# A graph network on one core: the attention layer's last sum and layer norm, taken in seven steps inside the dense stage

## The reference, cut to what matters

```python
x = _layernorm(x + _L0_gnn_ref(x, ..., src, dst, edge_type_40))     # attention
x = _layernorm(x + _L1_gnn_ref(x, edge_index, W_l, W_r))             # mean of the neighbours
x = _layernorm(x + _L2_gnn_ref(x, edge_index, edge_weight, ...))     # three graph convolutions
x = _layernorm(x + _L3_gnn_ref(x, edge_index, edge_attr_64, ...))    # filtered messages
```

## Time and profile before

| | us |
|---|---|
| median of three runs | 9683.03 |
| the profiled execution's own time | 9686.6 |
| its span, from the first to the last instruction | 9685.1 |
| TensorE matmuls busy | 7655.3 (79%) |
| VectorE busy | 4238.9 (44%) |
| ScalarE busy | 3170.6 (33%) |
| GpSimd busy | 5527.7 (57%) |
| mean granted TensorE clock, as a share of full speed | 0.874 |

### The profile page before, as it was taken

The page is one execution under the profiler, slowest core; times in us unless marked ns, Lnnn a source line. Parts: engine busy times, 40 slices in busy tenths (PEclk is TensorE's granted clock), DMA queues, the critical chain, the costliest instruction groups (busy, mean ns, idle before and its releaser), DMA issues. The chain is left out here.

```text
span 9685.1 us, 154107 instructions
## 1 busy us (share of the span) xinstructions
PE 7655.3 (79%) x38400; PEld 4785.0 (49%) x38401; DVE 4238.9 (44%) x9974; ACT 3170.6 (33%) x5260; POOL 5527.7 (57%) x5296
## 2 busy tenths in 40 slices
PE   1598888888888576665655899999999888888786
PEld 0354444444444365555554444444444656656564
DVE  6887777774443366666666100000000323323223
ACT  0012234566555476655554000000000233233322
POOL 4788888877776000000000667777775477777775
PEclk6899999999999766666666999999999999999998
DMA  4223445566666443333222899999999322222222
GB/s 108 76 90 118 147 150 186 196 215 234 212 213 211 153 134 119 114 104 100 93 90 68 311 338 335 339 335 343 324 355 329 116 77 77 77 78 77 78 77 66
DMA packets 563179, 1661.59 MB, mean 172 GB/s; under 512 B 115313, under 2 KB 312029, under 8 KB 519494
## 3 DMA queue, kind: packets, MB, share of 16 engines
q1 hardware_dynamic: 324442, 1129.76, 33.5%
q0 software_dynamic: 206976, 473.99, 16.5%
q10 hardware_dynamic: 31536, 54.94, 1.6%
HBM read 1174.46 MB, written 483.82 MB: 171 GB/s over the span
## 5 line engine op out<-in xcount | busy, mean ns | idle before, releaser
L907 PE MATMUL wide<-ring 128*128 128x392 bf16 x14112 | 2498.4, 339 | 501.3 <-DVE ring L837 260.9
L527 POOL DMA_INDIRECT z_got<-z_table,z_idx x1568 | 2114.5, 1349 | 596.4 <-issue 430.9
L907 PEld LDWEIGHTS wide<-ring 128*128 128x128 bf16 x14112 | 1407.8, 100 | 1591.7 <-issue 822.8
L1589 POOL DMA_INDIRECT l_rows<-h_table,l_recs x1568 | 1558.9, 994 | 630.1 <-issue 477.5
L1498 POOL DMA_INDIRECT sorted_recs<-dn_rec_in,type_f x1568 | 1520.0, 969 | 654.0 <-issue 470.9
L1042 POOL DMA_DIRECT2D rows<-z_edges x196 | 103.5, 528 | 2049.3 <-PE wide L362 1838.3
L1401 PE MATMUL wide<-stream,X 128*128 128x512 f32 (+1 forms) x2548 | 1045.5, 570 | 63.0 <-DMA stream<-c_dense 58.8
L373 PE MATMUL wide<-rows,onehot 128*128 128x130 f32 x3904 | 869.7, 411 | 245.8 <-DVE A L390 245.8
L373 PEld LDWEIGHTS wide<-rows,onehot 128*128 128x128 f32 x3904 | 805.3, 314 | 304.3 <-DVE A L390 304.3
L373 PE MATMUL wide<-l_rows,l_onehot 128*128 128x128 f32 x3904 | 587.2, 313 | 357.2 <-DVE X L391 357.2
L1688 DVE TENSOR_TENSOR l_rows<-l_filters,l_rows 128x1024 f32<-128x1024 f32 x196 | 240.2, 1226 | 1330.7 <-DMA l_rows<-h_table,l_recs 1313.2
(11 more groups left out here) (252 smaller groups left out, 8327.1 us busy)
## 6 DMA issues: line engine op xcount, KB each, us to landing
stream<-w_dense SPq DMA_DIRECT2D x252, 1792.0 KB
stream<-c_dense SPq DMA_DIRECT2D x84, 1792.0 KB
z_edges<-z_got POOLq DMA_DIRECT2D x196, 528.0 KB
rows<-z_edges POOLq DMA_DIRECT2D x196, 528.0 KB, 3.8
dst_bc<-in_dst_row SPq DMA_DIRECT2D x196, 512.0 KB, 3.7
c_dense<-A SPq DMA_DIRECT2D x49, 1568.0 KB
w_dense<-A SPq DMA_DIRECT2D x49, 1568.0 KB
c_dense<-H SPq DMA_DIRECT2D x49, 1568.0 KB
```

The source lines that it names most:

```text
L527: e.indirect_dma_start(out=z_got[:, s, t, :], out_offset=None, in_=z_table, in_offset=bass.IndirectOffsetOnAxis(ap=z_idx[:, s, t:t + 1], a ...
L907: ins = e.matmul(banks[:, bass.ds(to[v], 1), int(m > 0), 0:WC].rearrange("p a x -> p (a x)"), lhsT=slots[:, k, m * P:(m + 1) * P], rhs=slo ...
L1589: e.indirect_dma_start(out=rows[:, k, t, :], out_offset=None, in_=h_table, in_offset=bass.IndirectOffsetOnAxis(ap=recs[:, k, t, R_DST:R_DS ...
```

## The change

The two blocks of point 3 are gone. Their work is done in the dense block, by VectorE ahead of its own loop over the chunks, in seven pieces of seven node blocks. A piece is split in two: `add_attention(s)` goes up to the variance and raises `s_spread`; ScalarE takes the square root of that piece's seven variances and raises `s_root`; `normalize_x(s)` waits for that, normalizes the seven blocks and raises `s_x0`. `add_attention(s)` stands before `normalize_x(s - 1)`. In chunk 0 alone TensorE waits for `s_x0` before each of its seven steps. The square roots stand on ScalarE behind the first four loads of records and before its first copy of transposes (L1443 of the kernel before). SP's list and GpSimd's are unchanged; both begin with the dense block, and so now before this work and not after it. `rden` moves to the memory of the dense stage.

```diff
-        rden = sb("rden", [P, NB], of=edges)
-        A0 = A_(SW_)
-        with nc.Block() as block:
-            @block.vector
-            def _(e):
-                e.tensor_scalar(rden[:, :], A0[:, :, F], TINY, None, ALU.max)
-                e.tensor_scalar(rdeg[:, :], A0[:, :, MW], 1.0, None, ALU.max)
-                e.drain()
-                e.reciprocal(rden[:, :], rden[:, :])
-                e.reciprocal(rdeg[:, :], rdeg[:, :])
-                e.drain()
-                for b in range(NB):
-                    e.scalar_tensor_tensor(out=Xv[:, b, :], in0=A0[:, b, 0:F], scalar=rden[:, b:b + 1],
-                                           in1=Xv[:, b, :], op0=ALU.mult, op1=ALU.add)
-                e.drain()
-                e.tensor_tensor(Xv, Xv, bias["L0_gnn_bias_w"][:, :].unsqueeze(1).to_broadcast([P, NB, F]), ALU.add)
-                e.drain()
-        layernorm("l0n", None)
         release_semaphores()
...
+        s_spread, s_root, s_x0 = sem("dn_spread"), sem("dn_root"), sem("dn_x0")
...
                         for k in range(KQ):
                             b = s * KQ + k
+                            if i == 0 and k == 0:
+                                e.wait_ge(s_x0, s + 1)
...
+                    if i == 0:
+                        for s in range(NS):
+                            e.wait_ge(s_spread, s + 1)
+                            e.activation(rstd[:, s * KQ:(s + 1) * KQ], rstd[:, s * KQ:(s + 1) * KQ], ACT.Sqrt
+                                         ).then_inc(s_root, 1)
...
+                def add_attention(s):
+                    bs = slice(s * KQ, (s + 1) * KQ)
+                    for b in range(s * KQ, (s + 1) * KQ):
+                        e.scalar_tensor_tensor(out=Xv[:, b, :], in0=A0[:, b, 0:F], scalar=rden[:, b:b + 1],
+                                               in1=Xv[:, b, :], op0=ALU.mult, op1=ALU.add)
+                    e.drain()
+                    e.tensor_tensor(Xv[:, bs, :], Xv[:, bs, :],
+                                    bias["L0_gnn_bias_w"][:, :].unsqueeze(1).to_broadcast([P, KQ, F]), ALU.add)
+                    e.drain()
+                    for b in range(s * KQ, (s + 1) * KQ):
+                        e.bn_stats(stats[:, b, :], Xv[:, b, :])
+                    e.drain()
+                    for b in range(s * KQ, (s + 1) * KQ):
+                        e.bn_aggr(mv[:, b, :], stats[:, b, :])
+                    e.drain()
+                    e.tensor_scalar(rstd[:, bs], mv[:, bs, 1], EPS, None, ALU.add).then_inc(s_spread, 1)
+
+                def normalize_x(s):
+                    bs = slice(s * KQ, (s + 1) * KQ)
+                    e.wait_ge(s_root, s + 1)
+                    e.reciprocal(rstd[:, bs], rstd[:, bs])
+                    e.drain()
+                    for b in range(s * KQ, (s + 1) * KQ):
+                        ins = e.tensor_scalar(Xv[:, b, :], Xv[:, b, :], mv[:, b, 0:1], rstd[:, b:b + 1],
+                                              ALU.subtract, ALU.mult)
+                    ins.then_inc(s_x0, 1)
+
...
+                add_attention(0)
+                for s in range(1, NS):
+                    add_attention(s)
+                    normalize_x(s - 1)
+                normalize_x(NS - 1)
+                e.drain()
                 for c in range(NCH):
```

More of the change, by code:

```diff
@@ L1299, in build_program @@
         dvar = sb("dvar", [P, 4], of=dense)
+        rden = sb("rden", [P, NB], of=dense)
+        A0 = A_(SW_)
         agg_bank, lin_bank, own_bank, turn_x, turn_r = (bank[0], bank[1]), bank[2], bank[3], bank[4], bank[5]
@@ L1467, in normalize @@
                     return ins
+                def add_attention(s):
[23 more added lines that the diff above has]
+                    ins.then_inc(s_x0, 1)
+                e.tensor_scalar(rden[:, :], A0[:, :, F], TINY, None, ALU.max)
+                e.tensor_scalar(rdeg[:, :], A0[:, :, MW], 1.0, None, ALU.max)
+                e.drain()
+                e.reciprocal(rden[:, :], rden[:, :])
+                e.reciprocal(rdeg[:, :], rdeg[:, :])
+                e.drain()
+                add_attention(0)
[3 more added lines that the diff above has]
+                normalize_x(NS - 1)
+                e.drain()
                 for c in range(NCH):
```

## The result

The changed kernel takes 9647.5 us (median of five runs, 9630.5 to 9656.54) against 9685.68 us of the kernel before in the same session (five runs). The ratio is 0.9961, with a 95% interval of 0.995 to 0.9972: 38.2 us or 0.4% faster.

The account below looks back on a forecast made before the run. TensorE was taken to bound the dense stage, idle while VectorE worked alone before it. Chunk 0 ending at 5368.0 instead of 5406.2 us gains 38.2, so 9683.0 - 38.2 = 9645 us, range 9638 to 9662.

Parts of the forecast that it names:

- The start of the dense block: After the attention layer's last add (L390): dense block and its loads start 1.12 us later, at 5304.3 us.
- One piece: VectorE's work on seven node blocks: 7.5 us, 5.4 for `add_attention` and 2.1 for `normalize_x`; seven pieces 52.5 us.
- When X comes free: `s_x0` first rises at 5318.5 us, then every 7.5 us to the sixth at 5356.0; the seventh at 5358.1.
- What TensorE makes of it: Chunk 0: steps of 6.0 us, the first 2.5 longer, four pauses of 0.5 to 1.5 us, end at 5368.0.
- What moves with it: Loads, records and scatter start 48.5 us earlier; nothing is late, though GpSimd pauses some 20 us.
- The price not shown: VectorE's pieces beside GpSimd's scatters and full DMAs: cost between nothing and 31 us, taken as nothing.
- The range: Total time from 9638 us, if VectorE set no pace, to 9662 us, covering one late fetch and parts of rivals.
- rival 4: Dense stage: loads cannot follow TensorE's earlier pace and the gain is given back; up to 9664 us, chance 0.03.
- Rival 1: Chunk 0: pauses keep TensorE at the low clock; gain only 3.5 us, 9680 us, chance 0.02.
- Rival 2: VectorE's pieces: GpSimd's scatters block VectorE for up to 31 us; gain 11.1 us, 9672 us, chance 0.03.
- Rival 3: VectorE's pieces stall on late instruction fetches: one 9659 us (chance 0.04), two 9674 (0.02), four 9703 (0.03).

Follow-up runs that it names:

- x4: Changed kernel, but VectorE's work left uncut in 49-block instructions inside the dense block, with TensorE waiting once for all of it: 9681.41 us, interval 93.6 us.
- x3: Changed kernel, but TensorE waits before its first matmul of chunk 0 until all seven pieces are done: 9682.17 us, interval 100.0 us.
- x6: Changed kernel, but each piece is normalized right behind its own add, not after the next one's: 9646.45 us, interval 63.9 us.
- x7: Changed kernel, but GpSimd begins its scatter only after the last piece is done: 9660.89 us in one run, interval 65.2 us.
- x5: Changed kernel, with the seven bn_stats of each piece done three times over to lengthen the pieces: 9669.63 us, interval 87.0 us.
- x8: Changed kernel, with the bias row added by GpSimd in the attention stage and the last normalize done by ScalarE: 9655.56 us, interval 55.5 us.
- x9: Changed kernel, with only the normalize moved to ScalarE, on a slower chip: 10993.1 us, ratio 0.998 to the kernel before, interval 72.6 us.
- x11: The kernel of x9 again, on a chip like the first: 9657.58 us, ratio 0.9958 to the kernel before, interval 56.1 us.
- x10: The changed kernel run again on the slower chip of x9: 10953.84 us, ratio 0.9936 to the kernel before, interval 65.2 us.

## Why the prediction was right

The prediction was 9645 us and a gain of 38.2; measured were 9647.5 us and 38.2. That both gains read 38.2 is luck: the 95% interval of the measured one goes from 27 to 48 us. The profile is the closer test, with 37.7 us of the interval (103.0 - 65.2, before rounding) for 38.2. By the steps of the prediction:

- **The start of the dense block.** 1.12 us behind L390 were taken, the first load was issued 5315.86 - 5314.87 = 0.99 us behind it.
- **One piece.** 7.5 us were put together from sevenths of the long rows, a line for the bias row, and the gaps; 7.49 was measured, the bias row at 1.09 for 1.11. x4 and x3 confirm the claim that the cut costs something that VectorE can pay. Its size was read too small: "four more" sets 52.5 against some 48 us that include the two reciprocals. Like with like, against the 46.9 us from 5304.85 to 5351.70, the pieces of the prediction cost 5.6 us more, and 6.4 were measured (x3 over x4). The sum of the gain doesn't use that number.
- **When X comes free.** 15.3 us behind L390 in the working, 15.5 in the profile, then every 7.5 us. The root cost nothing (0.21 us on ScalarE, under VectorE's next add); x6, where it isn't hidden, shows what it would cost: 0.38 us in each piece.
- **What TensorE makes of it.** Four pauses were forecast and four came. The low clock at the start cost less (28 matmuls in 13.76 us, 1.5 us over their pace where 2.5 were taken), so the first pause was 1.23 and not 0.5. It made no difference, because the chunk ends at the sixth piece plus two steps: 64.8 us behind L390 in the working, 65.2 measured.
- **What moves with it.** A pause of some 20 us was forecast for GpSimd behind its first 32 scatters, and none came: the next records were loaded from 5365.65 us on, and the 33rd scatter started 0.31 us behind the 32nd. Nothing in the sum hung on it. The waits for loads in the dense stage stayed near 12 us (13.5, the answer to the earlier trace rows):

```profile
PE wide L1388 <- DMA stream<-w_dense: 13.5, 3, 5.0
```

- **The price not shown.** Nothing was taken, and in the interval it was nothing. Products took 343 to 352 ns beside the scatter and 341 to 350 without it; one `tensor_scalar` in each piece was longer (x7).
- **The range.** Its low end isn't what its terms give: 9683.0 - 42.2 - 4.4 is 9636.4 and not 9638. The 9664 of rival 4 follows from no row. The measured time lies well inside either way.

Rival 1, the low clock, fell in its own profile: from 5334 us on the granted clock was 1.00 through all pauses of 0.8 to 1.25 us.

```profile
5348.00:5355.00 7.00, 5.75 (x14) 2.37 (x13) 6.62 (x32) 0.21 (x1) 5.61 (x5) 1.00 0.81 257
```

x5 makes the clock fall and shows that it comes back within a step, as the prediction argued. What a fall would cost at pieces of 7.5 us was not tested: x5's spells made a step up to 3.1 us longer (9.31 for 6.25), which fits into its 10.55 us, while the prediction took 1.5 and a pause here is 1.25. Rival 2, GpSimd blocking VectorE, fell for the scatter and not for GpSimd at large: x8 has it at full size, for an instruction that computes. The Trainium skill, "SBUF — State Buffer", section "Who interferes with whom", states the exclusive lock; x8's 13.76 us agree with it. Who came first can't be read there: VectorE's row starts 0.34 us ahead of GpSimd's, and yet it is the one that stood. In the scatters of 2.0 us VectorE came first, and GpSimd waited. But where a scatter had started first, VectorE's products ran on unblocked (x7's rows), so a scatter doesn't block them as x8's instruction did. Rival 3, instruction fetches behind the loads, fell for this kernel: in the whole stretch (5315 to 5381 us) four packets of instructions came, and no row of a piece has a gap. Its effect, VectorE idle inside the pieces, does appear once, in x9, where it cost 16.5 us of the interval (72.6 for the 56.1 of x11); whether late fetches were its cause isn't shown.

Rival 4, loads that can't follow, did not happen in any run: in no profile of the changed kernel or its variants does a load end a wait of TensorE in chunk 0, x9 and x10 on the slower chip included.

What the prediction did not see is the size of chance. Its range took a run's spread as 4.4 us to a side, from three runs, and used it for the low end alone; the five runs of the changed kernel span 26 us, and the profiles put the scatter of single runs into the build stage, far ahead of the change.

## What to carry to other kernels

When one engine works alone between two stages and the next stage takes its data block by block, cut the work at the next stage's own steps and put it in the same block: the gain is the length of the shorter of the two, less what the last pieces and their steps stick out and what the cut itself costs (6.4 us here). Work it out from the last pieces and not from the first, and once the pieces are longer than the consumer's step, spend effort on the piece (another engine for a part of it), not on its order. Before work is given to an idle engine, ask what it blocks: GpSimd had 38 us free and cost some 11 by using 13.

## What the runs showed of the hardware that was not expected

- One VectorE instruction, 0.16 us elsewhere, stood for 13.76 us beside a GpSimd `tensor_tensor` of 13.39 us (x8). Beside GpSimd's indirect DMAs nothing like it happened; there a scatter that started inside VectorE's run of two-operand products took 2.0 us for 0.97.
- Pauses up to 1.62 us left the granted clock at 1.00 (x6); pauses of 2.78 and 3.86 us were followed by stretches at 0.52 and 0.50, and the one of 2.63 us by a slow step too (x5). With VectorE's pieces at 10.55 us such a stretch cost next to nothing, since TensorE waited for them anyway.
- The same kernel took 9684 us on one chip and 11011 us on another. On the latter TensorE stood still between the matmuls of a step, 449.5 us in 324 pauses of x9's dense stage, with the DMA engines nearly idle in a burst of them (0.08, x10). The stage's 240 to 260 GB/s for 337 look like slow loads, yet TensorE's waits for loads were 8.3 us; the cause of the pauses is open. On that chip a version that is faster elsewhere (x9) was not, by idle time in VectorE's pieces whose cause is open.
